# The second layer's experts: gated rows scattered by token and choice, then loaded in six blocks instead of gathered

## The reference, cut to what matters

```python
def _L1_ffn_ref(x, Wg, W1, b1, Wo, bo):          # x: 32 x 100 x 256, W1: 8 x 1024 x 256
    TOP_K, EPS = 2, 1e-09
    E = Wg.shape[0]
    gate_logits = jnp.einsum('btd,ed->bte', x, Wg)
    gate_scores = jax.nn.softmax(gate_logits, axis=-1)
    topk_val, topk_idx = jax.lax.top_k(gate_scores, TOP_K)
    topk_val = topk_val / (topk_val.sum(axis=-1, keepdims=True) + EPS)
    comb = (jax.nn.one_hot(topk_idx, E, dtype=x.dtype) * topk_val[..., None]).sum(axis=-2)
    out = jnp.zeros_like(x)
    for e in range(E):
        h = jnp.einsum('btd,hd->bth', x, W1[e]) + b1[e]
        a, b = jnp.split(h, 2, axis=-1)
        g = a * jax.nn.sigmoid(b)                # the gated row: 512 numbers
        eo = jnp.einsum('bth,dh->btd', g, Wo) + bo
        out = out + eo * comb[..., e:e + 1]
    return out
# ... attention and experts of layer 0, attention of layer 1 ...
x = x + _L1_ffn_ref(_layernorm(x, axis=-1), ...)
```

## Time and profile before

| | us |
|---|---|
| median of 3 runs | 1670.88 (1667.91 to 1671.15) |
| the profiled execution | 1672.24 |
| its span | 1670.4 |
| PE busy in the span | 1475.5 (88%) |
| routing and experts of layer 1 in the span | from about 1343 to the end |

### The profile page before, as it was taken

How to read it: one execution, slowest core, us unless ns; L and a number is a source line. 1 busy time by engine, 2 the same in 40 slices (tenths; PEclk the granted TensorE clock), 3 DMA queues, 4 the chain that set the end, 5 groups by cost and what they waited for, 6 DMA issues and landing times. The chain is left out here.

```text
span 1670.4 us, 50633 instructions
## 1 busy us (share of the span) xinstructions
PE 1475.5 (88%) x17398; PEld 1232.2 (74%) x17399; DVE 1071.5 (64%) x2260; ACT 909.6 (54%) x1658; POOL 934.3 (56%) x1145
## 2 busy tenths in 40 slices
PE   5999999999996499999599999999999646999676
PEld 4777777777774499999478888888888524888565
DVE  3767676677673566666346776777777577777544
ACT  3677777777774255555266656656665323333233
POOL 3576676676673166665457667666666305333263
PEclk8999999999997699999799999999999757999889
DMA  5111211111100455554302222321110042333375
GB/s 146 47 63 59 82 50 59 59 26 31 34 18 10 143 186 185 188 188 158 91 27 76 71 95 65 93 72 49 40 49 25 18 139 94 127 129 131 125 237 181
DMA packets 66640, 153.15 MB, mean 92 GB/s; under 512 B 11490, under 2 KB 36254, under 8 KB 59974
## 3 DMA queue, kind: packets, MB, share of 16 engines
q1 hardware_dynamic: 56254, 124.20, 22.9%
q0 software_dynamic: 10320, 28.07, 5.8%
HBM read 119.93 MB, written 32.29 MB: 91 GB/s over the span
## 5 line engine op out<-in xcount | busy, mean ns | idle before, releaser
L1017 DVE TENSOR_REDUCE a_mx<-a_SM 100x2 bf16<-100x722 f32 x384 | 351.3, 915 | 202.4 <-PE a_SM L459 199.1
L737 ACT ACTIVATE a_Pr<-a_ST 120x1600 f32<-120x1600 f32 (+3 forms) x192 | 225.1, 1172 | 125.5 <-PE a_ST L491 123.4
L459 PE MATMUL a_SM<-a_KT,a_QM 32*100 32x362 f32 x768 | 152.3, 393 | 26.1 <-DVE a_mx L1017 25.9
L501 PE MATMUL a_M<-a_Pr,a_V 120*32 120x100 f32 (+3 forms) x4608 | 174.9, 255 | 0.0
L787 POOL TENSOR_TENSOR a_rstd<-a_ve,a_powers 100x1 f32<-100x1 f32 x192 | 119.0, 620 | 96.4 <-DVE a_ve L986 94.7
L1530 POOL TENSOR_TENSOR e_hT_low<-e_hT,e_hT_high 128x1024 fp32r<-128x1024 f32 x32 | 105.5, 3296 | 91.7 <-ACT e_hT_high L1613 91.7
L501 PEld LDWEIGHTS a_M<-a_Pr,a_V 120*32 120x32 f32 (+3 forms) x4608 | 134.7, 119 | 21.5 <-issue 12.5
L862 POOL TENSOR_TENSOR a_cl<-a_ct,a_ch 128x724 fp32r<-128x724 f32 x62 | 107.3, 1730 | 43.1 <-DVE a_o L1059 43.1
L386 PE MATMUL a_M<-a_wvh,a_ch 128*120 128x256 f32 (+1 forms) x384 | 124.0, 323 | 4.4 <-ACT a_KF L623 4.4
L852 POOL TENSOR_TENSOR a_KL<-a_KF,a_KT 128x724 fp32r<-128x724 f32 x64 | 111.6, 1744 | 26.9 <-ACT a_KT L631 15.8
L1563 PE MATMUL e_PH<-e_xT,e_wS 128*128 128x128 f32 x1024 | 122.5, 279 | 2.1 <-DVE e_xT L1653 2.1
(11 more groups left out here) (225 smaller groups left out, 4176.0 us busy)
## 6 DMA issues: line engine op xcount, KB each, us to landing
e_wS<-in_E_w SPq DMA_DIRECT2D x32, 1024.0 KB
a_ct<-in_ctx SPq DMA_DIRECT2D x64, 362.0 KB, 3.2
w<-in_E_w SPq DMA_DIRECT2D x16, 1024.0 KB, 6.0
gated_rows<-g_hs SPq DMA_DIRECT2D x57, 256.0 KB
keep_rows<-a_keep SPq DMA_DIRECT2D x64, 100.0 KB
tile_rows<-e_y SPq DMA_DIRECT2D x32, 128.0 KB, 1.7
X<-in_E_b SPq DMA_DIRECT2D x1, 4096.0 KB
x_rows<-X SPq DMA_DIRECT2D x32, 100.0 KB
```

What stands on the lines that cost most here:

```text
L459: last = nc.tensor.matmul(SM[0:LQ, half, 0:LKP], QM[b.p][rows, chunk, m, :], KT[b.p][rows, chunk, :], start=True, stop=True)
L501: last = nc.tensor.matmul(M0[VW * j:VW * (j + 1), g * LQ:(g + 1) * LQ], V[b.p][0:n, kt, h, :], Pr[0:n, kt, POS[h] * LQ:(POS[h] + 1) * LQ], ...
L737: nc.scalar.activation(Pr[0:n, s, :].rearrange("p (r q) -> p r q", r=GROUPS), ST[0:n, :, 0:PER * LQ], ACT.Exp, scale=SCALE).then_inc(exp_d ...
L1017: V_.tensor_reduce(pair, SM[0:LQ, :, 0:LK], AX_X, ALU.max).then_inc(max_done, 1)
```

## The change

In `routing` the two lists of slots are gone (two transposes, two copies, and a transfer of half the size are left), and DVE works out a second number per slot, `places`: the row 100 + token of the first choice, or 100 + 3200 + token of the second, in a DRAM tensor with 13796 rows. The batch numbers are counted from one (`seqs_up`), so that a slot without a pair shows a zero and gets a row of its own behind the others (`slot_no`).

In the first phase POOL gathers with a column of `toks` as it stands, without the copy, and stores each tile's gated rows by scatter to `places`. SP stores nothing there. `hs` has four buffers instead of two. All POOL and SP loops are written out.

In the second phase the rows of `gated` lie by token, so SP loads them: 12 transfers (two choices, six blocks of 1, 1, 2, 4, 8 and 9 steps), one behind the other, into memory that the weights had. They are issued once all scatters have landed and PE is through with the weights. `combine` writes into the loaded rows themselves.

```diff
@@ routing
-            by_token = sb("by_token", [LQ, 4, NB])
-            by_seq = sb("by_seq", [NB, 4, LQ])
+            by_token = sb("by_token", [LQ, 2, NB])
+            by_seq = sb("by_seq", [NB, 2, LQ])
...
-                if layer == 1:
-                    V_.tensor_copy(by_token[:, k, :], den[:]).then_inc(flat_ready, 1)
-                    dve.wait_ge(flat_ready, 3 + k)
...
-                link(V_.tensor_scalar(second[:], seq_f[:], float(NB), None, ALU.is_ge))
-                link(V_.scalar_tensor_tensor(seq_f[:], second[:], float(-NB), seq_f[:], ALU.mult, ALU.add))
-            link(V_.tensor_copy(tok_f[:], PS[:, 2, NT:2 * NT]))
-            link(V_.scalar_tensor_tensor(tok_f[:], seq_f[:], float(LQ), tok_f[:], ALU.mult, ALU.add))
-            link(V_.tensor_copy(env["toks"][:, 0:NT], tok_f[:]))
+                link(V_.tensor_scalar(second[:], seq_f[:], float(NB + 1), None, ALU.is_ge))
+                link(V_.scalar_tensor_tensor(seq_1[:], second[:], float(-NB), seq_f[:], ALU.mult, ALU.add))
+                link(V_.tensor_copy(tok_1[:], PS[:, 2, NT:2 * NT]))
+                link(V_.scalar_tensor_tensor(tok_f[:], seq_1[:], float(LQ), tok_1[:], ALU.mult, ALU.add))
+                link(V_.tensor_scalar(tok_f[:], tok_f[:], float(-LQ), 0.0, ALU.add, ALU.max))
+                link(V_.tensor_copy(env["toks"][:, 0:NT], tok_f[:]))
+                link(V_.scalar_tensor_tensor(tok_f[:], seq_f[:], float(LQ), tok_1[:], ALU.mult, ALU.add))
+                link(V_.scalar_tensor_tensor(seq_1[:], tok_f[:], float(LQ), slot_no[:], ALU.is_lt, ALU.mult))
+                link(V_.tensor_tensor(tok_f[:], tok_f[:], seq_1[:], ALU.add))
+                link(V_.tensor_copy(env["places"][:, 0:NT], tok_f[:]))
@@ gated_tiles
-    RING = 4
+    BLOCKS = (0, 1, 2, 4, 8, 16, FLAT)
...
@@ sync
-            def store(j, p):
-                sp.wait_ge(h_ready, j + 1)
-                sp.dma_start(t["gated"][bass.ds(j * 128, 128), :], hs[p][:]).then_inc(g_stored[p], 16)
...
+            for p in range(DEEP):
+                sp.wait_ge(g_stored[p], 16 * len(range(p, NT, DEEP)))
+            sp.wait_ge(sig_done, NT)
+            sp.wait_ge(h_ps, NT)
+            for i, (b, end) in enumerate(zip(BLOCKS, BLOCKS[1:])):
+                for k in range(2):
+                    rows = t["gated"][LQ + k * TOK:LQ + (k + 1) * TOK].rearrange("(p i) f -> p i f", i=FLAT)
+                    sp.dma_start(rows_at(k, b, end - b), rows[:, b:end]).then_inc(g_loaded[i], 16)
...
+            for b in range(FLAT):
                 store_out(b, b % DEEP)
                 if b + DEEP < FLAT:
                     load_x(b + DEEP, b % DEEP)
@@ gpsimd
-                nc.gpsimd.tensor_copy(gidx[p][:], env["toks"][:, bass.ds(j, 1)]).then_inc(gidx_ready, 1)
...
-            def pair_of_rows(b):
...
+            def gather(j):
+                if j >= DEEP:
                     pool.wait_ge(x_ps, j - (DEEP - 1))
+                nc.gpsimd.indirect_dma_start(xs[j % DEEP][:], None, t["keep"],
+                                             bass.IndirectOffsetOnAxis(env["toks"][:, j:j + 1], 0)
+                                             ).then_inc(rows_loaded[j % DEEP], 16)
+            def place(j):
+                pool.wait_ge(h_ready, j + 1)
+                nc.gpsimd.indirect_dma_start(t["gated"], bass.IndirectOffsetOnAxis(env["places"][:, j:j + 1], 0),
+                                             hs[j % DEEP][:], None).then_inc(g_stored[j % DEEP], 16)
             for j in range(DEEP):
+                gather(j)
+            for j in range(NT):
+                if j + DEEP < NT:
+                    gather(j + DEEP)
+                place(j)
```

More of the change, by code:

```diff
@@ L1305, in _ @@
                 if k == 1:
-                    pe.wait_ge(flat_ready, 4)
-                    for a in range(4):
+                    pe.wait_ge(flat_ready, 2)
+                    for a in range(2):
                         last = nc.tensor.transpose(PS[0:NB, 3, a * LQ:(a + 1) * LQ], by_token[:, a, :],
@@ L1732, in gated_tiles @@
         ssum = sb("ssum", [128, FLAT])
-        where = sb("where", [128, 2, FLAT], I32)
-        gidx = [sb(f"gidx{p}", [128, 1], I32) for p in range(DEEP)]
         xs = [sb(f"xs{p}", [128, D]) for p in range(DEEP)]
@@ L1751, in gated_tiles @@
         small_loaded = sem("small_loaded")
-        turns = env["pool_turns"]
-        gidx_ready = sem("gidx_ready")
         rows_loaded = [sem(f"rows_loaded{p}") for p in range(DEEP)]
@@ L1910, in down @@
                 last.then_inc(y_ps, 1)
-            turn(0, 0, 0)
-            for b in range(2):
-                turn(b + 1, 1 - b, 1)
-                down(b, b, b)
-            with pe.Fori(1, FLAT // 2) as i:
-                for p in range(2):
-                    turn(i * 2 + (p + 1), 1 - p, 2)
-                    down(i * 2 + p, p, 2)
-            down(FLAT - 1, (FLAT - 1) % 2, 2)
+            turn(0)
+            for b in range(FLAT):
+                if b + 1 < FLAT:
+                    turn(b + 1)
+                down(b)
         @block.scalar
@@ L2035, in _ @@
             dve.wait_ge(env["second_loaded"], 16 * len(env["second"]))
-            for j in range(2):
+            for j in range(DEEP):
                 tile(j, j, 0, j, False)
-            with dve.Fori(1, (NT - 2) // 2) as i:
-                for p in range(2):
-                    tile(i * 2 + p, p, i, 2, False)
-            for j in range((NT - 2) // 2 * 2, NT):
-                tile(j, j % 2, j // 2, 2, j + 2 >= NT)
-            def combine(b, p, r, far):
+            with dve.Fori(1, (NT - 2) // DEEP) as i:
+                for p in range(DEEP):
+                    tile(i * DEEP + p, p, i, DEEP, False)
@@ L2045, in combine @@
+            for j in range((NT - 2) // DEEP * DEEP, NT):
+                tile(j, j % DEEP, j // DEEP, DEEP, j + 2 >= NT)
+            share0 = env["flat"][:, 0, :]
+            def combine(b):
                 dve.wait_ge(part_ready, b + 1)
-                if far >= 2:
-                    dve.wait_ge(gT_ps, b - 1)
-                dve.sem_inc(dve_turns, 1)
-                V_.scalar_tensor_tensor(comb[p % 2][:], GR[p][:, 0, :], share0[:, bass.ds(b, 1)], GR[p][:, 1, :],
+                V_.scalar_tensor_tensor(row_at(0, b), row_at(0, b), share0[:, b:b + 1], row_at(1, b),
@@ L2070, in _ @@
-            for b in range((FLAT - 2) // DEEP * DEEP, FLAT):
+                V_.tensor_tensor(y[p][:], PY[:, b % 2, 0:D], xr[p][:], ALU.add).then_inc(y_ready, 1)
+            combine(0)
+            combine(1)
+            for b in range(FLAT):
                 if b + 2 < FLAT:
-                    combine(b + 2, (b + 2) % RING, (b + 2) // RING, 2)
-                total(b, b % DEEP, b // DEEP, DEEP)
+                    combine(b + 2)
+                total(b)
     end_stage(nc, sems)
```

162 lines of the change are left out of this document (62 added, 100 removed).

## The result

The changed kernel takes 1685.26 us in the median of 5 runs (1683.04 to 1689.7), the kernel before 1670.88 in 5 runs beside them (1667.91 to 1673.95); the ratio is 1.009, with a 95% interval of 1.0075 to 1.0105. It is slower, by 0.9%. I had forecast 1665.0, with a range of 1656 to 1681.

What follows compares the result with a forecast made beforehand. PE's own work was taken to bound the first phase, waits for gathers and transfers the second. Last block at 1615.0 plus 49.5 us gave a span of 1664.5 against 1670.4 (-5.9), median 1665.0, range 1656 to 1681.

Steps and rivals of the forecast that it cites:

- Routing and first gathers: Ahead of the first phase: routing +0.4 us, first gathers -0.9 us with DVE's weight splits moving along, -0.5 in all.
- First phase, 0: First phase: the added scatters cost nothing, a tile stays at 3.02 us, set by PE's own work alone.
- Both covers: First phase: POOL works 2.5 of 3.02 us a tile; gather j+5 lands 1.4 to 2.4 us before PE needs it.
- Rival 2: First phase: POOL sets the pace, by a scatter over 1.45 us or gather over 5.1; up to 1710 us, chance 0.13.
- Last rows to first load: Between the phases: the last scatter takes 3.1 us and lands at 1577.3, then SP issues the 12 loads.
- The block of loads: Second phase: 13.1 MB in 12 loads take 35.4 us (bounds 32.7 to 43.7), the last there at 1615.0.
- Where the gain stops: Second phase: step 4's residual load queues behind all 12 loads, so steps 4 to 24 end after 1615; then +49.5 us.
- the cold step: Second phase: PE's first step after some 20 us idle runs at granted clock 0.50 and takes 4.5 us.
- Rival 1: Second phase: residual rows get through between the blocks, so loads are hidden behind PE; median 1642 us, chance 0.09.
- Steps 0 to 3: Second phase: they have their residual rows from the start and run as the blocks land, from about 1581.
- The sum: Whole kernel: 1615.0 + 49.5 = 1664.5 us span against 1670.4, so -5.9 us.

Runs made afterwards that it cites:

- pair_short: Changed kernel without the scatter (SP stores the tiles), plus a 32-row software gather straight behind each gather; 1666.0 us in one run.
- best: Changed kernel with the wait of `aligned`, residual rows loaded apart between smaller blocks, outputs written over them; 1658.5 us, ratio 0.9936 to the kernel before.
- xr_apart: Changed kernel with residual rows of steps 4 to 24 loaded between the blocks into their own region; 1683.95 us, ratio 1.0093 to the kernel before.
- two_gathers: Changed kernel with SP storing the tiles and a gather into an unread buffer in the scatter's place; 1680.31 us in one run.
- to_slots: Changed kernel with the scatter's row numbers replaced by consecutive ones, the second phase loading from there; 1681.35 us in one run.
- busy_long: Changed kernel with SP storing the tiles and a plain GpSimd copy of 128x768 elements in the scatter's place; 1664.94 us in one run.
- mid_gather: Changed kernel without the scatter (SP stores the tiles), its one gather a tile held until DVE's low columns; 1657.64 us in one run.
- aligned: Changed kernel with the scatter of tile j held until PE has transposed the rows of tile j + 3; 1669.78 us, ratio 1.0002 to the kernel before.

## Why the prediction was wrong

**Routing and first gathers: the sum came out by luck.** Forecast -0.5 in all, and the first product on `hs` starts at 1403.50, not 1403.89: 0.4 earlier. But DVE's first instruction of the second layer's routing starts 0.73 us earlier in this execution (1342.66 against 1343.39), before anything that was changed. From there to GpSimd's way out of the barrier behind routing (line 107, at 1380.99 after and 1381.27 before) it is 38.33 us and not 37.88: +0.45, as forecast (+0.4). From there to the first product it is 22.51 and not 22.62: -0.1, where -0.9 was forecast. The second gather does land 2.15 us earlier (1387.59 against 1389.74), but the last of DVE's weight splits ahead of the first product ends only 0.4 us earlier (1402.05 against 1402.44), so the splits didn't move with the gathers, as the prediction assumed.

**First phase, 0: wrong, and the whole of the miss.** It was +22.1 for 54 tiles. The working asked whether GpSimd has the time (it has: 0.97 us a scatter forecast, 0.987 measured) and whether gather j+5 lands before it is needed (it does; PE never waits for `g_xs`). Both covers held (the first was added up as +3.9 where its terms give 3.83). The step that failed is the sentence that nothing but PE's own work sets the time there and that other engines matter only if they fall behind it, with the 0 that followed from it. PE's work goes on by its signals to ACT and DVE, and these have a slack of their own that I never worked out. The kernel before, first phase, in order of time (lines 1861 and 1934 are the transposes and ACT's copy of them, 1988 DVE's low columns, for which the next transposes wait):

```profile
1433.52 0.38 PE L1861 MATMUL g_PX<-kept_ident,g_xs 128*128 128x128 f32 x2
...
1434.02 0.39 ACT L1934 ACTIVATE g_xTh<-g_PX 128x256 fp32r<-128x256 f32 x1 [1.83 <-PE g_PX L1861]
...
1435.05 0.42 DVE L1988 TENSOR_TENSOR g_xTl<-g_PX,g_xTh 128x256 fp32r<-128x256 f32 x1
...
1436.53 0.38 PE L1861 MATMUL g_PX<-kept_ident,g_xs 128*128 128x128 f32 x2
```

The low columns are ready at 1435.47 and wanted at 1436.53. An increment of the transposes may be 1.06 us late and no more. One of 1 us is just hidden, as mostly in `pair_short`; one of 3 us is a stall of 2 us.

**The view of waits was misread, and with it the warning missed.** The prediction took DVE's four waits for something without a name (14.9 us) for the store of four steps ago, and what stands ahead of it says that on one core such waits are for transfers. Neither holds. The second phase of the kernel before has two gathers a step, and it shows the very thing that the changed kernel moved into its first phase (line 1900 is a step's transposes, 1963 ACT's evacuation of them, 1908 its products, 2058 the output):

```profile
1636.76 0.60 PE L1900 MATMUL g_PT<-kept_ident,g_comb 128*128 128x128 f32 x4
1637.20 1.89 PE L1908 MATMUL g_PY<-g_wo,g_gT 128*128 128x256 f32 x8
...
1642.03 0.60 ACT L1963 ACTIVATE g_gT<-g_PT 128x512 f32<-128x512 f32 x1 [2.50 <-remote]
...
1644.12 0.42 DVE L2058 TENSOR_TENSOR g_y<-g_PY,g_xr 128x256 f32<-128x256 f32 x1 [2.86 <-remote]
```

The transposes end at 1637.36 and ACT, free from 1639.53, starts at 1642.03; the semaphore events have PE's increment at 1641.92. The products end at 1639.09; DVE's waits for the store and for `xr` are over at 1641.3, and the increment of the products comes at 1644.10. It is the same in all four waits: DVE starts 0.02 to 0.03 us behind increments seen at 1611.04, 1620.92, 1630.85 and 1644.10, which are 3.0 to 5.0 us behind the ends that the profile has for the products. ACT has seven more such waits there, in the same view of waits as the earlier trace rows but not read by the prediction, and each ends with an increment of PE's transposes that is 1.6 to 4.6 us late:

```profile
ACT g_gT L1963 <- remote: 15.8, 7, 3.5
```

Without gathers, in `best`, ACT starts 0.04 us behind the transposes in 23 of 25 steps, and in the changed kernel in 24. What the first phase lost is this effect, carried there; how much of the second phase's gain is that increments come in time again was not measured apart.

**Rival 2: right in sign, wrong in mechanism.** It gave 1678 to 1710, and 1685 is in that, but by a scatter over 1.45 us or a gather over 5.1 us, and neither occurred. "No row shows it" was said of the scatter's duration; rows did show what two software transfers in a row do to others.

**Last rows to first load: 1.2 us too short.** Forecast was 3.3 us from the last `hs` to the first load, measured 4.5 (1596.07 to 1600.53). The last scatter starts 1.7 us behind its rows, where others start 0.3 behind; it lands in 2.73, where I took 3.1.

**The block of loads: 3.5 us too slow.** From the first load until the residual rows of step 4 are there, forecast 38.9 us (37.6 to the last block and 1.3), measured 35.4. The 411 GB/s of the last 20 us are above the 401 of the earlier trace rows that was my upper bound. (The prediction says of its stretches that they lie between the two figures that it cites; 325 and 327 lie below both.)

**Where the gain stops: right, and incomplete.** The wait at `g_xr` of step 4 is there (12.7 us in DVE's waits), the cold step 1.12 + 3.41 against 4.5, and from the landing to the end 48.7 us against 48.2. Rival 1 is out. What I missed has no price in the changed kernel, but `xr_apart` had to pay for it: the stores of steps 0 to 3 stand in the same queue, and steps 4 to 7 wait for them too. Steps 0 to 3 didn't run as early as I said (first transpose at 1610.57, 10 us behind the first load, since ACT takes the rows of step 2 ahead of step 0); that was hidden under the queue.

**The sum.** Against the forecast span of 1664.5 the span of 1684.7 is +20.2: first phase +21.8 from its first product, start +0.1, last rows to load +1.2, loads -3.5, after them +0.5 (0.1 is rounding). The second phase as a whole came out within 2 us, in part because its terms missed to either side.

## What to carry over

- A phase in which one engine is busy all the time still runs on signals, and a wait without a name in the profile may be for one of them. Before adding work on another engine there, work out how late each signal of the busy engine may be, not only how busy the other engine gets.
- A transfer that stands behind a large block in a queue isn't only the next load: every store in that queue waits too, and with it every buffer that is to be used again. Here, taking the loads alone out of the block's way brought nothing, and taking loads and stores out brought 10 us.
- A first-order cause is soon found by replacing the added instruction by its neighbours in kind (same transfer to other rows, another transfer, plain work of the same length) and reading one stretch in each profile; the total time of single runs, which moved here by 7 us with the start alone, would have blurred it.

## What the runs showed of the hardware

- With a second software transfer (one whose descriptors GpSimd makes) in each tile of 3 us, increments of TensorE are seen up to 3.6 us late (3.27 in the changed kernel, 3.59 in `pair_short`), while all of DVE's and ACT's that the changed kernel's trace recorded beside them came within 0.02 us. With two such transfers a step in the second phase of the kernel before, they are up to 5.0 us late. In the first phase the stalls are there with a gather in the scatter's place (182.1 us for the 54 tiles, `two_gathers`) and with other addresses (181.9, `to_slots`), and not with plain work of 0.82 us (161.7, `busy_long`) or with one transfer a tile (161.8, `mid_gather`); moving the scatter within the tile takes most of the loss away (169.1, `aligned`).
- What holds the increments is open. In `pair_short` the delay of the transposes' increment grows, in every second tile by some 0.1 us, from 0.16 at 1420.9 to 0.92 at 1463.1, and stays near there; in the changed kernel it jumps between 0 and 3.3 us. In both, GpSimd's instructions stand at the same places within the tile before the first late increment as in it, so the places of the instructions don't explain the onset; what does, no row shows. From what rate of such transfers on it begins (a second one in every other tile, say) was not run either.
- Twelve loads in one queue reached 411 GB/s over 20 us (1616 to 1636), in which runs of 16 and 18 KB a partition moved, and residual and output rows of 1 KB at the end.
